# Row maxima of layer 1's one-head blocks: the causal mask moves from a TensorE product into VectorE's reduction

## What is computed

```python
q = (x @ Wq.T).reshape(B, S, 2 * H, hd).transpose(0, 2, 1, 3) * scaling
k = (x @ Wk.T).reshape(B, S, 2 * H, hd).transpose(0, 2, 1, 3)
scores = jnp.einsum('bhqd,bhkd->bhqk', q, k)
causal = jnp.triu(jnp.full((S, S), -jnp.inf, dtype=scores.dtype), 1)
attn = jax.nn.softmax(scores + causal, axis=-1)
attn = attn.reshape(B, H, 2, S, S)
w = attn[:, :, 0] - lam * attn[:, :, 1]
o = jnp.einsum('bhqk,bhkd->bhqd', w, v)
```

## Time and profile before

| | us |
|---|---|
| median of 3 runs | 2462.93 (2460.99 to 2463.0) |
| the profiled execution | 2466.63 |
| its span, from first to last instruction | 2464.5 |
| stage of layer 1's heads, TensorE's first product to VectorE's last maximum | 1947.8 to 2275.2 |
| VectorE / ScalarE / TensorE busy over the whole span | 1533.1 / 1363.7 / 2156.1 |

### The profile page before, as it was taken

How to read it: one execution, slowest core, us unless ns; L and a number is a source line. 1 busy time by engine, 2 the same in 40 slices (tenths; PEclk the granted TensorE clock), 3 DMA queues, 4 the chain that set the end, 5 groups by cost and what they waited for, 6 DMA issues and landing times. The chain is left out here.

```text
span 2464.5 us, 49127 instructions
## 1 busy us (share of the span) xinstructions
PE 2156.1 (87%) x15930; PEld 1268.1 (51%) x15930; DVE 1533.1 (62%) x3120; ACT 1363.7 (55%) x2226; POOL 697.1 (28%) x577
## 2 busy tenths in 40 slices
PE   3763899999999999999938999999998399999587
PEld 2331677777777777777724444444443144444132
DVE  2663788888888888888743434434432566666354
ACT  1441566666666666666724554454553166666464
POOL 1443544444444444444401122222123000000000
PEclk9885999999999999999968999999998699999799
DMA  5333111111111111111011122122211222222221
GB/s 179 104 114 91 33 36 33 33 33 33 33 33 33 33 33 33 33 32 32 20 31 60 65 94 67 56 90 68 94 69 34 73 91 90 89 89 69 90 90 35
DMA packets 156366, 151.01 MB, mean 61 GB/s; under 512 B 83656, under 2 KB 113874, under 8 KB 155026
## 3 DMA queue, kind: packets, MB, share of 16 engines
q1 hardware_dynamic: 150930, 148.11, 20.5%
q10 hardware_dynamic: 5376, 2.12, 0.3%
HBM read 96.08 MB, written 54.12 MB: 61 GB/s over the span
## 5 line engine op out<-in xcount | busy, mean ns | idle before, releaser
L1141 ACT ACTIVATE prob<-prob,neg_max_h 128x640 f32<-128x640 f32 x512 | 424.3, 829 | 329.4 <-DVE neg_max_h L1039 329.0
L1039 DVE CUSTOM_DVE_ANT_0 prob<-pair,pair_mask 128x640 f32<-128x640 f32 x512 | 418.9, 818 | 153.2 <-PE pair L956 153.0
L1102 POOL TENSOR_TENSOR a_full<-rot_c,rot_s 128x512 f32<-128x512 f32 x128 | 163.0, 1273 | 501.9 <-DVE rot_s L1026 501.9
L1622 PE MATMUL pair<-hid,down_w 128*128 128x512 f32 x640 | 295.6, 607 | 3.3 <-ACT hid L1548 3.3
L1046 DVE TENSOR_TENSOR prob<-prob 128x128 f32<-128x128 f32 x512 | 273.6, 534 | 0.5 <-ACT prob L1141 0.5
L1548 ACT ACTIVATE hid<-pair,up_b 128x512 f32<-128x512 f32 x320 | 198.6, 692 | 106.2 <-PE pair L1602 105.9
L912 PE MATMUL turn<-ident,prob 128*128 128x128 f32 x1024 | 250.4, 275 | 0.1
L912 PE MATMUL outsum<-ident,prob 128*128 128x128 f32 x1024 | 249.7, 275 | 0.5 <-ACT prob_t L1149 0.5
L1920 ACT ACTIVATE prob_h<-pair 128x512 f32<-128x512 f32 (+1 forms) x352 | 186.7, 561 | 102.7 <-PE pair L1820 98.5
L1875 DVE TENSOR_REDUCE row_max<-pair 128x1 f32<-128x384 f32 (+3 forms) x352 | 199.4, 634 | 32.6 <-PE pair L1795 31.9
L1622 PEld LDWEIGHTS pair<-hid,down_w 128*128 128x128 f32 x640 | 121.9, 193 | 150.9 <-issue 130.7
(11 more groups left out here) (270 smaller groups left out, 4324.1 us busy)
## 6 DMA issues: line engine op xcount, KB each, us to landing
o_d<-out_sb SPq DMA_DIRECT2D x64, 256.0 KB, 2.0
w_all<-w_d SPq DMA_DIRECT2D x8, 2048.0 KB, 10.8
vx_d<-vx SPq DMA_DIRECT2D x8, 1024.0 KB, 4.9
val_h<-vx_d SPq DMA_DIRECT2D x32, 256.0 KB
qs_d<-part_q SPq DMA_DIRECT2D x48, 128.0 KB
ks_d<-part_k SPq DMA_DIRECT2D x48, 128.0 KB
num<-o_d SPq DMA_DIRECT2D x24, 256.0 KB
den<-o_d SPq DMA_DIRECT2D x24, 256.0 KB
```

Source lines behind the costliest of these rows:

```text
L1039: nc.vector.tensor_tensor_reduce(prob[s % 4][:, :], pair[:, cols], pair_mask[:, cols], -1.0, 3.0e38, ALU.add, ALU.min, neg_max[par][:, s:s ...
L1102: nc.gpsimd.tensor_tensor(a_full[h % 2][:, :], rot_c[h % 2][:, :], rot_s[h % 2][:, :], ALU.add).then_inc(a_steps.sem, 1)
L1141: nc.scalar.activation(prob[s % 4][:, :], prob[s % 4][:, :], ACT.Exp, bias=neg_max[par][:, s:s + 1], scale=-1.0).then_inc(exp_done.sem, 1)
L1622: mm = nc.tensor.matmul(out_ap, down_w[:, EXPERTS[i], c, :], hid[i % 2][:, c, :], start=(c == 0 and i != 1), stop=(c == HC - 1 and i != 0))
```

## The change

For the eight one-head items of a group (items 3 to 10) the mask product on TensorE is left out and the score product opens the accumulation itself. On VectorE the reduction of such an item is replaced by one fused operation: score plus mask, times -1, with a minimum over the columns into row_max1; the masked scores go to one of two new SBUF tiles, masked1, which nobody reads. The mask is the slice of pair_mask whose last 128 columns are the triangle. Ahead of each fused operation stand a wait for the operation two before (the same masked1 tile) and an increment of a new semaphore, h1_scores_seen, for which nobody waits. The items of several heads stay as they are.

```diff
@@ allocations of layer 1's heads
+        masked1 = [sb(f"masked1{i}", [P, S], F32, h1_scope) for i in range(2)]
+        h1_scores_seen = sem("h1_scores_seen")
@@ max_item, TensorE
-                nc.tensor.matmul(dst[:, :, i0:w], identb[:, :], mask_low.unsqueeze(1).broadcast_to([P, heads, P]),
-                                 start=True, stop=False, skip_group_check=True)
+                if heads > 1:
+                    nc.tensor.matmul(dst[:, :, i0:w], identb[:, :], mask_low.unsqueeze(1).broadcast_to([P, heads, P]),
+                                     start=True, stop=False, skip_group_check=True)
                 for x in range(heads):
                     mm = nc.tensor.matmul(dst[:, x, :], q_h1[k][0:KM, h0 + x, i0:w], k_h1[k][0:KM, h0 + x, 0:w],
-                                          start=False, stop=(x == heads - 1), skip_group_check=True)
+                                          start=(heads == 1), stop=(x == heads - 1), skip_group_check=True)
@@ row_maxima, VectorE
                     v.wait_ge(h1_max_ready.sem, h1_max_ready.at(NM * n + m + 1))
-                    src = bank[EXP_BANKS + (NM * k + m) % MAX_BANKS][:, 0:heads * w].rearrange("p (h n) -> p h n", h=heads)
+                    scores = bank[EXP_BANKS + (NM * k + m) % MAX_BANKS][:, 0:heads * w]
+                    if heads == 1:
+                        v.wait_ge(h1_max_used.sem, h1_max_used.at(NM * n + m - 1))
+                        v.sem_inc(h1_scores_seen, 1)
+                        ve.tensor_tensor_reduce(masked1[m % 2][:, 0:w], scores, pair_mask[:, S - w:S], -1.0, 3.0e38,
+                                                ALU.add, ALU.min, row_max1[:, h0, ib:ib + 1]).then_inc(h1_max_used.sem, 1)
+                        continue
+                    src = scores.rearrange("p (h n) -> p h n", h=heads)
                     ve.tensor_reduce(row_max1[:, h0:h0 + heads, ib], src, AX_X, ALU.max, negate=True
                                      ).then_inc(h1_max_used.sem, 1)
```

## The result

| | before | after |
|---|---|---|
| median of 12 runs each, us | 2463.24 | 2457.14 |
| lowest to highest, us | 2460.47 to 2466.48 | 2450.28 to 2462.65 |
| profiled span, us | 2464.5 | 2455.9 |
| mean granted clock | 0.943 | 0.941 |

The ratio of the run times is 0.9971, with an interval of 0.9962 to 0.998: 7.1 us faster (5 to 9), where 6.8 were forecast.

A forecast was written before the change was run, and what follows sets the result against it. TensorE bounds, busy 9.90 of a 10.40 us round. Four counting masks gain 0.22 us a round, 6.9 us over 31 rounds, less 0.1 ahead of the loop: 6.8 us, giving 2456.1 us; range 2452 to 2464.

The forecast's parts named there:

- The slot of a mask product: On TensorE, each removed mask product frees 0.056 us; eight are 0.45 us a round.
- Only m3, m4, m5 and m10 count: On TensorE, only the masks of maximum items 3, 4, 5 and 10 shorten the round, by 0.22 us.
- The stop before e5: TensorE idles before exponential item 5 until ScalarE ends item 3; grows from 0.30 to some 0.5 us, swallowing four masks.
- the copy of the sums: On ScalarE between exponential items 2 and 3; item 3 waits for it and so moves by 0.17 us only.
- Banks: Maximum item 9 on TensorE needs item 5's bank, free at 2106.03, wanted at 2106.05; any delay is hidden.
- The fused operation, 0.48 and 0.61 us: VectorE's step for 384 and 512 columns, 0.015 us more each; with the accumulator read exposed, 0.56 and 0.69.
- The held first operation: On VectorE, maximum item 3 would wait for all before it, about 0.1 us, without changing the sum.
- Cover of what the maxima feed: Between the padding behind maximum item 10 and the turn on TensorE: 1.4 us, 1.2 after the change.
- the slower rival: VectorE's fused operations don't follow closely and set the round, above 0.70 us for 384 columns: 10.9 us, 2479 us; chance 0.13.
- No-gain: Fused price near 0.70 us, or only maximum item 10's mask counts: 2 us gained, 2461 us; chance 0.15.
- more-comes-through rivals: TensorE's full 0.45 us a round arrives, if exponential item 3 runs without the copy ahead: 14 us, 2449 us; chance 0.04.
- Ahead of the loop: Group 0's maxima on VectorE stand uncovered: eight fused operations at 0.015 us more, 0.1 us lost.

The follow-up runs named there:

- run 2: Kernel before with only maximum items 3, 4, 5 and 10 changed: round 10.163 us, against 10.400 before and 10.163 in the fully changed kernel.
- run 1: Kernel before with only maximum items 6 to 9 changed: round 10.400 us, against 10.400 before.
- run 7: Changed kernel with ScalarE's copy of the sums moved from behind exponential item 2 to behind item 1: round 9.997 us, ratio to before 0.9956.
- run 8: Kernel before with ScalarE's copy of the sums moved from behind exponential item 2 to behind item 1: round 10.193 us, ratio to before 0.9977.
- run 3: Changed kernel with the fused operations on VectorE but the mask products kept on TensorE: round 10.400 us.
- run 9: Changed kernel plus a one-column VectorE copy of pair_mask into a spare tile ahead of maximum item 0: round 10.166 us.
- run 5: Changed kernel plus an extra 128-column VectorE add ahead of each fused operation: round 10.420 us.
- run 6: Changed kernel plus an extra 256-column VectorE add ahead of each fused operation: round 11.333 us.
- run 10: Changed kernel with the edits of run 7 and run 9 together: round 9.870 us, ratio to before 0.9933.

## Why the prediction was right, point by point

- *The slot of a mask product, 0.056 us.* Four of them were forecast to give 0.22 us a round, and 0.237 came: 0.059 each, as for the mask of m3 (2103.45 to 2103.51). Shown by run 2 against before.
- *Only m3, m4, m5 and m10 count.* Shown by runs 1 and 2, which give none and all of it.
- *The stop before e5 takes the rest.* The mechanism held (run 1: 0.30 to 0.53 us), and the copy of the sums is its cause (runs 7 and 8). The size in the changed kernel was off: 0.35 us instead of some 0.5, because of the next point.
- *Banks.* This step was incomplete. I worked out m9 against m5 and named m8 against m4, but not m7 against m3. m3's maximum is done 0.12 us later than I had it, m7 waits 0.14 us for its bank (2089.89 to 2090.03), and this is the time that the stop before e5 lacks. It cost nothing only because the stop lay behind it, which was luck as far as m7 goes, since my text had not looked; in run 7 the same wait cost 0.13 us a round.
- *The fused operation, 0.48 and 0.61 us.* Right to a hundredth, and the accumulator read was free, the lower of my two bounds. Run 3 shows that the loop doesn't see what it costs more.
- *The held first operation.* I took it from the Trainium skill (VectorE: DVE Perf Modes, "Two Vector instructions with no wait between them"), by which an instruction waits for the end of all before it when its input from a memory starts in another quadrant (group of 32 partitions) than the last one read there. No row of before could show it. The trace agrees: m3 starts 0.12 us late, at m2's end, and m4 to m9 don't; a read from partition 0 ahead of it (run 9) removes the delay. My text gave it 0.1 us and no effect, which holds for the rounds of the changed kernel, and neither for run 7 nor for the first round (below).
- *Cover of what the maxima feed, and the point where the slower rival decides.* The cover exists, but 0.70 us was the wrong point: the banks decide first, at 0.60 (an estimate from the rows, borne out by run 5); the turn decides in run 6. My upper bound of 0.56 was below both, so the sum didn't suffer.
- *No-gain and more-comes-through rivals.* Neither happened. The condition that I named for more to come through, e3 without the copy ahead of it, was not enough. With the copy moved in both kernels the change is worth 10.193 - 9.997 = 0.196 us a round, less than the 0.237 with the copy in the way, as m7's wait for m3's bank is then in the open. With m3 no longer held as well it is 10.193 - 9.870 = 0.323, more than 0.237 but not the 0.45 of all eight masks: the masks of m8 and m9 stand between e3's product and e5 and still fall into the stop.
- *Ahead of the loop.* 0.1 us was forecast; the first round grew from 8.54 to 8.77 us, 0.23. The traces separate two parts: m3 starts 2.00 us behind m0 instead of 1.89, so it is held here too and nothing covers it, and the padding starts 6.48 us behind m0 instead of 6.25, of which the other 0.12 are the forecast's eight items. The clock has a share in this round as well: in run 3 the padding also starts at 6.48, but the granted clock around the turn was 0.94 instead of 0.50, and the round took 8.55.
- *The total.* My text counted 31 equal rounds; the first two are not (8.54 and 10.11 us before) and gained nothing. That 31 x 0.22 and 29 x 0.237 are both 6.9 us is luck: a slot taken too small and two rounds too many cancel. Those two even got longer, from 8.54 to 8.77 and from 10.11 to 10.22. That makes 6.5 us from the first to the last m0, against a forecast of 6.8; the runs say 7.1 (5 to 9), which can't tell the two apart.

What stays open: the second round varies by up to 1.3 us between executions, together with its mean granted clock (10.02 us at 0.94 in run 9, 11.23 us at 0.82 in run 10). Why the clock comes up at another place each time wasn't tried.

## What to carry to other kernels

Before counting removed work, find the stops of the bounding engine in one round and ask of each removed instruction which stop it lies in front of: work in front of a stop that another engine ends is worth nothing, and here that halved the gain. Then look at what makes the stop; moving one copy by one place on ScalarE gave nearly as much (run 8) as taking eight products off TensorE. It made those products worth more (0.32 us a round for 0.24) only once the next limit, m3's late start, was gone too. And when banks go round, check every handover, not only the last: the one left out (m7 on m3) was the next limit.

## What the runs showed of the hardware

An accumulator read costs no time of its own even between two fused operations that both write the accumulator: starts 0.48 us apart for 384 columns in the changed kernel, with the 0.08 us record of the read beside the next operation. (The plain reduction is 0.47 us.) And a VectorE operation whose SBUF input starts at partition 0 waited for its forerunner's end after an earlier operation had read SBUF at partition 96, with three operations that read only PSUM in between; 0.12 us, gone with a one-column read in idle time (run 9). I had expected the first to be possible and had not expected that the second would ever set the round, as it does in run 7.
